# Decoder block on one core: 1/v is applied to the decayed scores on ScalarE, where GpSimd applied it to the context rows

## The reference

```python
def _L0_xattn_ref(Q, K, V):
    B, S, d = Q.shape
    x = jnp.einsum('bsd,btd->bst', Q, K) / d ** 0.5
    Dm = _decay_matrix(S)
    Dm = Dm / jnp.sqrt(jnp.sum(Dm, axis=1))
    x = x * Dm
    v = jnp.maximum(jnp.abs(jnp.sum(x, axis=-1)), 1.0)
    x = x / v[:, None, :]
    return jnp.einsum('bst,btd->bsd', x, V)
...
x = _layernorm(x + _L0_attn_ref(x, L0_attn_Wk, L0_attn_Wv, L0_attn_Wo, L0_attn_freqs), axis=-1)
x = _layernorm(x + _L0_xattn_ref(x, ctx_1024, ctx_1024), axis=-1)
x = _layernorm(x + _L0_ffn_ref(x, L0_ffn_router_w, L0_ffn_up_proj, L0_ffn_down_proj), axis=-1)
```

## Time and profile before

| | us |
|---|---|
| median of 3 runs | 265.36 |
| lowest, highest | 264.54, 266.08 |
| the profiled execution's own time | 262.09 |
| its span (first to last instruction) | 260.3 |
| PE, PEld busy in it | 206.9, 181.5 |
| DVE, ACT, POOL busy in it | 162.7, 111.1, 143.0 |
| granted TensorE clock, mean | 0.929 |

### The profile page before, as it was taken

How to read it: one execution, slowest core, us unless ns; L and a number is a source line. 1 busy time by engine, 2 the same in 40 slices (tenths; PEclk the granted TensorE clock), 3 DMA queues, 4 the chain that set the end, 5 groups by cost and what they waited for, 6 DMA issues and landing times.

```text
span 260.3 us, 5161 instructions
## 1 busy us (share of the span) xinstructions
PE 206.9 (79%) x1365; PEld 181.5 (70%) x1366; DVE 162.7 (62%) x534; ACT 111.1 (43%) x277; POOL 143.0 (55%) x132
## 2 busy tenths in 40 slices
PE   8669899999999997756999999999999999300000
PEld 8557798898888996745888888888888888200000
DVE  5856888888887684954554544554545454118992
ACT  2323144244234113641454545454545454425665
POOL 0074674674675310565577777777777774416340
PEclk9999999999999999979999999999999999955555
DMA  7964665765641012802222323233232341089323
GB/s 217 383 260 149 239 188 197 231 229 184 225 122 43 0 44 89 276 3 60 81 89 92 101 86 101 89 99 101 85 101 89 102 91 66 9 271 317 139 90 151
DMA packets 20129, 35.73 MB, mean 137 GB/s; under 512 B 2861, under 2 KB 11312, under 8 KB 20112
## 3 DMA queue, kind: packets, MB, share of 16 engines
q1 hardware_dynamic: 16368, 26.21, 30.0%
q0 software_dynamic: 3744, 9.31, 11.8%
HBM read 27.12 MB, written 9.31 MB: 140 GB/s over the span
## 4 chain that ended last, share of the span: by engine, by line
PE 65%; DVE 17%; issue 6%; POOL 4%; DMA 4%; ACT 2%; SPq 1%; DVEq 0%; ACTq 0%; POOLq 0%
PE p_c L545 14%; PE p_v L545 7%; PE p_y L467 6%; PE p_v L411 4%; PE p_y L571 4%; PE p_r L545 4%; PE p_a L545 3%; PE p_s L545 3%; PE p_t L584 3%; PE p_s L451 3%; POOL space L992 3%; PE p_c L427 3%; DVE space L838 3%; PE p_r L495 2%; PE p_a L486 2%
## 5 line engine op out<-in xcount | busy, mean ns | idle before, releaser
L545 PE MATMUL p_c<-w_hi,parts 128*128 x104 | 34.7, 414 | 0.0
L1016 POOL DMA_INDIRECT y_dram<-x1T,scatter_now x26 | 26.3, 1013 | 11.8 <-issue 6.2
L996 POOL DMA_INDIRECT turns<-x_dram,gather_now x26 | 25.4, 979 | 12.6 <-issue 3.8
L983 POOL TENSOR_TENSOR w_lo<-keep,w_hi 128x1536 fp32r<-128x1536 f32 (+1 forms) x8 | 27.5, 3440 | 0.0
L810 DVE TENSOR_TENSOR parts<-p_y,parts 128x256 fp32r<-128x256 f32 x39 | 16.5, 424 | 17.4 <-ACT parts L912 17.4
L820 DVE TENSOR_TENSOR cs<-p_c,cs 128x256 f32<-128x256 f32 x26 | 11.0, 424 | 22.8 <-ACT cs L919 22.8
L970 POOL TENSOR_TENSOR space<-back 128x512 f32<-128x512 f32 x8 | 10.1, 1267 | 26.9 <-DVE back L704 26.9
L919 ACT ACTIVATE cs<-p_c 128x256 f32<-128x256 f32 x26 | 10.1, 387 | 24.8 <-PE p_c L545 24.8
L978 POOL TENSOR_TENSOR cs<-space,vinv 128x256 f32<-128x256 f32 x16 | 9.5, 613 | 18.3 <-DVE vinv L718 14.9
L545 PEld LDWEIGHTS p_c<-w_hi,parts 128*128 128x128 f32 x104 | 17.6, 189 | 2.4
L912 ACT ACTIVATE parts<-p_y 128x256 fp32r<-128x256 f32 x39 | 14.9, 381 | 8.6 <-PE p_y L571 8.5
(11 more groups left out here) (153 smaller groups left out, 551.4 us busy)
## 6 DMA issues: line engine op xcount, KB each, us to landing
keep<-in_weights SPq DMA_DIRECT2D x8, 768.0 KB, 4.4
space<-y_dram SPq DMA_DIRECT2D x16, 256.0 KB, 4.1
space<-in_xT SPq DMA_DIRECT2D x8, 256.0 KB, 3.5
keep<-in_x SPq DMA_DIRECT2D x8, 256.0 KB, 3.6
space<-in_ctxT SPq DMA_DIRECT2D x8, 256.0 KB, 2.8
space<-in_ctxt SPq DMA_DIRECT2D x8, 256.0 KB, 3.0
x_dram<-x SPq DMA_DIRECT2D x8, 256.0 KB, 2.2
keep<-x_dram SPq DMA_DIRECT2D x1, 2048.0 KB, 8.4
```

Of the source, the lines that this page charges most:

```text
L545: last = nc.tensor.matmul(dst, lhs[:, k, :], w[:].rearrange("p e n -> p (e n)")[:, bass.ds(start + col + k * width, width)], start=(n == 0 ...
L983: nc.gpsimd.tensor_tensor(w_lo[:, bass.ds(i, 1), :].rearrange("p a n -> p (a n)"), w_in[s], w_hi[:, bass.ds(i, 1), :].rearrange("p a n -> ...
L996: nc.gpsimd.indirect_dma_start(xs[s], None, x2_dram, bass.IndirectOffsetOnAxis(ap=gather_now[s][:], axis=0)).then_inc(xs_ok[s], 16)
L1016: nc.gpsimd.indirect_dma_start(y_dram, bass.IndirectOffsetOnAxis(ap=scatter_now[s][:], axis=0), ys[s], None, bounds_check=TOPK * N - 1, oo ...
```

## The change

The scores are now scaled, in a new tile `att_div`, by two ScalarE activations (one for each sequence of the pair, with `vinv` as a scale per partition). The two GpSimd multiplications that made `cs` are gone in the first stage. The weighted product takes `att_div` as weights and the context rows as they were loaded. Three waits go with it: the next context load waits for the product (`av_ok`) in place of `cs_ok`; TensorE waits for the context rows itself; and the load of x2 into `keep` waits for the last `w_lo`.

```diff
@@ decoder_block
+        att_div = sb("att_div", [P, 2, T])
@@ block.sync, step
                     load(cT_in, ctxT, cT_ok, i + 1, 1 - s)
                     if has(-1):
-                        sp.wait_ge(cs_ok, i)
+                        sp.wait_ge(av_ok, i)
                     load(c_in, ctxt, c_ok, i + 1, 1 - s)
@@ block.sync, behind the pipeline
             sp.sem_inc(x2_saved, 1)
 
+            sp.wait_ge(lo_ok, PAIRS)
+
             sp.dma_start(x2_keep.rearrange("p j n -> p (j n)").rearrange("p (j q d) -> p (j q) d", q=2, d=D),
@@ block.tensor, step
                 if has(-1):
                     keep_busy(idle[3], ident, 0)
+                    pe.wait_ge(c_ok[1 - s], 8 * (i - 1 - (1 - s)) + 16)
                     pe.wait_ge(cs_ok, i)
                     if has(-2):
                         pe.wait_ge(r2_ok, i - 1)
                     for q in range(2):
-                        last = nc.tensor.matmul(p_a[:, q, :], att[:, q, :], cs[:, q, :], start=True, stop=True)
+                        last = nc.tensor.matmul(p_a[:, q, :], att_div[:, q, :], c_in[1 - s][:, q, :], start=True, stop=True)
@@ block.scalar, step
                     nc.scalar.activation(vabs[:], rowsum, ACT.Abs).then_inc(vabs_ok, 1)
+                    act.wait_ge(vinv_ok, i)
+                    if has(-2):
+                        act.wait_ge(av_ok, i - 1)
+                    for q in range(2):
+                        last = nc.scalar.activation(att_div[:, q, :], att[:, q, :], ACT.Copy, scale=vinv[:, q:q + 1])
+                    last.then_inc(cs_ok, 1)
                 if has(0):
                     act.wait_ge(w_ok[s], 8 * (i - s) + 16)
@@ block.gpsimd, step
-                if has(-1):
-                    pool.wait_ge(c_ok[1 - s], 8 * (i - 1 - (1 - s)) + 16)
-                    pool.wait_ge(vinv_ok, i)
-                    if has(-2):
-                        pool.wait_ge(av_ok, i - 1)
-                    for q in range(2):
-                        last = nc.gpsimd.tensor_tensor(cs[:, q, :], c_in[1 - s][:, q, :], vinv[:, q:q + 1].to_broadcast([P, D]), ALU.mult)
-                    last.then_inc(cs_ok, 1)
-
                 if has(0):
                     pool.wait_ge(hi_ok, i + 1)
```

## The result

The changed kernel takes 270.45 us in the median of 4 runs (269.58 to 271.06), against 264.95 (263.60 to 266.08) for the kernel before. The two medians are 5.5 us apart; the recorded ratio is 1.024 with a 95% interval of 1.0194 to 1.0287, so 5 to 7.6 us slower. A second set gave 271.11 against 263.37, ratio 1.0268 (1.0213 to 1.0323). The profiled execution took 271.06, with a span of 268.9.

What follows compares the result with a forecast made beforehand. The prediction took a ring through GpSimd's `w_lo` and VectorE's x1 normalisation, held until `w_lo` ends, to bound the turn. +6.3 for the ring and -0.4 in turn 8 gave +5.9 on 265.36: 271.3 us, range 269.2 to 273.0.

Steps and rivals of the forecast that it cites:

- the ring: First stage: `vinv`, `cs`, `w_lo`, x1, transposes, scores, next `vinv`; as long as TensorE's turn or longer, so lengthening it lengthens turns.
- ring term: Turns 1 to 7: `vinv` to the end of `w_lo` takes 5.64 us each, against 33.2 us in all before: +6.3 us.
- Rival 1: First stage: the end of `w_lo` is no gate, TensorE is the bound; +0.8, 266.2 us; chance 0.07.
- Rival 2: First stage: VectorE is slowed beside `w_lo`, not stopped, so x1 moves with its own start; +2.1, 267.4 us; chance 0.05.
- The cover for `x2T`: ScalarE, behind `w_hi`: `x2T` and the logits product come 0.41 us late, less than x1's 0.9, so no added cost.
- The lengths of the first L655: VectorE's x1 normalisation beside `w_lo`: first instruction of each pair at some 1 us, x1 ending 0.47 behind `w_lo`.
- The gain at the end: Turn 8: without `cs` on GpSimd, VectorE's first L682 takes 0.26 in place of 0.64 us: -0.38 us.
- SyncE and the added waits: Context loads starting about 1 us later, the load waiting for the last `w_lo`, and TensorE's extra wait: cost nothing.
- rival 3: TensorE idles 0.6 us more a turn; one turn at half clock would cost up to 9 us: 280; chance 0.02.
- the main case: First stage: the ring grows and turn 8 gains; +5.9 us, 271.3 us, own range 269.3 to 272.9; chance 0.84.
- rival 4: First stage: `w_hi` not delayed, GpSimd's ring 1.3 us shorter, TensorE sets the turn; 1.6 less, 263.8 us; chance 0.02.

Runs made afterwards that it cites:

- all four lengths above: `vinv` to the end of `w_lo`, summed over turns 1 to 7: before 33.2, wait_only 36.3, add_only and changed kernel 39.8 to 39.9, scale_twice 44.0 us.
- w_hi_first: Changed kernel with `w_hi` moved ahead of the two scalings and their wait for `vinv` on ScalarE: 262.72 us, ratio 0.9955.
- wait_only: Kernel before with one added wait, `w_hi` on ScalarE also waiting for `vinv`, and no scalings: 267.01 us, ratio 1.0134.
- the quarters: Changed kernel with `w_lo` made by four GpSimd instructions of 384 columns in place of one of 1536: 269.76 us, ratio 1.0259.
- remove_only: Changed kernel without its two scalings, the product taking `att` and the context rows as they are: 262.11 us, ratio 0.9947.
- w_hi_early: Changed kernel with `w_hi` moved right behind `x1T` on ScalarE and `w_lo` also waiting for `vinv`: 261.78 us, ratio 0.9938.
- add_only: Kernel before with the two ScalarE scalings added ahead of `w_hi`, their result unread, and GpSimd's `cs` kept: 270.24 us, ratio 1.0247.
- scale_twice: Changed kernel with both scalings made twice, the first pair into a tile nobody reads: 275.00 us, ratio 1.0449.

## Why the prediction was right, and where it was off

The forecast was 271.3 us, +5.9 over the kernel before; the runs gave 270.45, +5.5 by the medians and +6.4 by the ratio. The profiled execution was forecast at 268.0 and took 271.06. Those 3.1 us are about 0.4 in the ring, 1.5 of the clock in turn 2, 0.4 at the start, 0.4 behind the stage and 0.3 outside the span. That the median came closer than this is partly luck: the sum had no term for the clock, and its ring term was 0.4 short.

- **What bounds the kernel.** Right. The ring through `w_lo` and x1 sets the turn. At all four lengths above the turns follow it one to one, and reordering alone (w_hi_first) takes the whole loss away. Rival 1, TensorE as the bound, falls with wait_only, in which `x2T` isn't late and the kernel is 3.5 us slower. Rival 2, a port shared in part, falls with the quarters.
- **The ring term**, +6.3: it measured 39.9 - 33.2 = 6.7. The scalings cost 394 ns each and `w_hi` starts 0.60 behind the first, as taken from L901. Off were the wakes: GpSimd's is 0.19 in the loop turns (70.96 to 71.15) and 0.08 in the others, where I had 0.10, and ScalarE's is 0.03 to 0.11, where I had 0.03.
- **The cover for `x2T`.** Right: it came 0.3 to 0.4 us late (2.01 and 2.09 us behind `vinv` in place of 1.70, since it starts 0.1 before `w_hi` is over), the logits' loads waited 0.5 to 0.6, and x1 was later still. I put TensorE's wait at 0.5; it was 0.75 to 0.97 from turn 2 on. In turn 5 the loader had waited 0.14 before, which I had not added, x1 came 1.01 later and not 0.93, and TensorE only 0.29 later and not 0.41: 0.14 + 1.01 - 0.29 = 0.86.
- **The lengths of the first L655**, some 1 us: they measured 1.17 to 1.44, and 1.84 in turn 1. The end of the pair, 0.47 to 0.48 behind `w_lo`, is as forecast in all seven turns, and that is what the sum used.
- **The gain at the end**, -0.38: it measured -0.39, and 19.13 to 19.15 us in remove_only, w_hi_first and w_hi_early, against 19.51 in add_only, which keeps `cs`.
- **SyncE and the added waits**, nothing: right. remove_only has them too and is not slower than before, and all behind the stage is within 0.4 us.
- **The clock.** Here the argument failed in part: the sum had it at nothing, and the sign that it named for rival 3, a clock under 1.00 before 100 us, is in the profile, beside the main case and not in its place. I compared a mean turn with the stretch at 20 to 30 us. Turn 1 is not like the others: TensorE already waited 1 us for x1 there, and the change made that 2.3. The clock fell, for 3.4 us and not for a turn, and cost 1.2 to 1.5 us in the profiles that have it, where the rival said up to 9. The price should have been read for the one turn with the longest wait.
- **A gain if `w_hi` were not delayed** (rival 4), -1.6: remove_only, which has no scalings, gave -1.4. w_hi_first gave -1.2 by the ratio but only 0.7 in its profile, with the scalings' price before `p_a` in it.

## What to carry to other kernels

Before work is moved to an engine with more idle time, look at what is queued behind the place where it goes: ScalarE was busy 43% of the span and had room, but what stood behind the new wait was the first link of a chain through GpSimd and VectorE. If the same instruction form has a spread of durations, such as 401 to 957 ns, look for what runs beside its long ones and ends with them; here that found a ring that the chain of waits showed as TensorE. And try the order before the engine: `w_hi` ahead of the wait costs a few moved lines.

## What the hardware showed

- A GpSimd tensor_tensor on SBUF holds up a VectorE tensor_scalar until the GpSimd instruction is over: 0.4 us alone, up to 1.84 in the changed kernel and 2.42 in scale_twice beside one of 3.4 us, and each of two waits for the end of a quarter of 1.0 us when it comes in four. This is the rule of the Trainium skill (SBUF — State Buffer, Who interferes with whom), and the traces agree with it for a GpSimd instruction that was there first. The other direction shows here only as the 0.04 to 0.10 us by which a quarter behind an L655 is longer than the others. A held L655 ends 0.15 us after the GpSimd instruction, where it takes 0.41 alone, so that some 0.26 us of it are done by then.
- A VectorE tensor_tensor with two SBUF inputs is held as well: the first L682 of turn 8 (L686 with the change) took 0.64 in the three kernels that have `cs` beside it (before, add_only, wait_only) and 0.26 in the others.
- GpSimd's start after a ScalarE result took 0.19 us in the register loop and 0.08 in turns that are written out.
- One idle stretch of TensorE of 2.3 to 2.4 us, in a stage that otherwise keeps it busy about nine tenths, came with 3.4 us at the lower clock level in three profiles out of three, which began between 0.3 us before TensorE went on and 1.3 us after; stretches of 1.85, 1.5 and 1.0 us at the same place had no fall.
